# One tile in 32 fetched row by row by SyncE and ScalarE instead of by a GpSimd gather

## The reference

```
h = max(layernorm(x), 0); x = x + sum over edges of norm * (h[src] @ W)            # layer 0
h = max(layernorm(x), 0); x = x + GRU(segment_sum(mlp([h[src], h[dst], e])), h)    # layer 1
h = max(layernorm(x), 0)
n = segment_sum(h[src], dst);  x = x + max(((1 + eps) h + n) @ W1 + b1, 0) @ W2 + b2   # layer 2
h = max(layernorm(x), 0)
m = segment_sum(h[src], dst) / max(count, 1)
x = x + max(m @ Wl.T + bl + h @ Wr.T, 0)                                           # layer 3
```

## Time and profile before

| | us |
|---|---|
| median of three runs | 11380.71 |
| the profiled execution | 11306.17 |
| its span, first to last instruction | 11304.4 |
| GpSimd busy | 7460.0 |
| TensorE busy | 5949.6 |
| VectorE busy | 3267.7 |
| ScalarE busy | 659.7 |
| layer two's edge stage, about 6281 to 8714 | 2433 |
| layer three's edge stage, about 8800 to 11251 | 2451 |

### The profile page before, as it was taken

How to read it: one execution, slowest core, us unless ns; L and a number is a source line. 1 busy time by engine, 2 the same in 40 slices (tenths; PEclk the granted TensorE clock), 3 DMA queues, 4 the chain that set the end, 5 groups by cost and what they waited for, 6 DMA issues and landing times. The chain is left out here.

```text
span 11304.4 us, 126194 instructions
## 1 busy us (share of the span) xinstructions
PE 5949.6 (53%) x34165; PEld 5515.0 (49%) x34166; DVE 3267.7 (29%) x4802; ACT 659.7 (6%) x1678; POOL 7460.0 (66%) x6808
## 2 busy tenths in 40 slices
PE   6566656666656777777777333333334333333334
PEld 5555555665656777777777322222223222222224
DVE  9343434334333323222233311111112211111111
ACT  3000000000001000000001000000000000000000
POOL 1888888888875555555654666666665566666665
PEclk6555555555556666666667655555556655555555
DMA  2333333333342111111111111111111111111111
GB/s 71 20 20 20 20 20 20 20 20 20 20 53 52 34 33 34 34 34 34 34 34 24 29 23 23 23 23 23 23 23 20 31 23 23 23 23 23 23 23 29
DMA packets 714529, 310.35 MB, mean 27 GB/s; under 512 B 623117, under 2 KB 627231, under 8 KB 714079
## 3 DMA queue, kind: packets, MB, share of 16 engines
q0 software_dynamic: 398640, 218.14, 16.1%
q1 hardware_dynamic: 314252, 90.77, 3.8%
q10 hardware_dynamic: 1572, 0.67, 0.0%
HBM read 223.75 MB, written 85.30 MB: 27 GB/s over the span
## 5 line engine op out<-in xcount | busy, mean ns | idle before, releaser
L969 POOL DMA_INDIRECT h_rows<-h_tab,idx x3322 | 3159.8, 951 | 1799.7 <-issue 960.3
L1521 PE MATMUL ps_seg<-hot,h_rows 128*64 128x128 f32 x6656 | 1475.9, 413 | 3231.8 <-DVE hot L1406 2979.7
L769 POOL DMA_INDIRECT parts_tab<-total,row_at x1661 | 2559.2, 1541 | 689.1 <-issue 491.2
L1521 PEld LDWEIGHTS ps_seg<-hot,h_rows 128*64 128x64 f32 x6656 | 1321.5, 220 | 3373.5 <-DVE hot L1406 1757.7
L969 POOL DMA_INDIRECT a_rows<-a_tab,idx x1661 | 1579.6, 951 | 1136.7 <-DVE pre L1119 564.7
L1450 DVE TENSOR_TENSOR acc_t<-acc_t,ps_seg 64x128 f32 x416 | 116.4, 280 | 3568.9 <-remote 1386.3
L1141 PE MATMUL ps_seg<-hot,act_rows 128*65 128x128 f32 x3328 | 752.3, 411 | 352.3 <-ACT act_rows L1214 256.7
L1141 PEld LDWEIGHTS ps_seg<-hot,act_rows 128*65 128x65 f32 x3328 | 660.8, 222 | 385.4 <-issue 375.9
L681 PE MATMUL ps_dst<-identb,relb 128*128 128x128 bf16 x1672 | 215.9, 310 | 1075.4 <-DVE relb L615 1075.4
L681 PEld LDWEIGHTS ps_dst<-identb,relb 128*128 128x128 bf16 x1672 | 161.0, 141 | 1111.5 <-DVE relb L615 1107.7
L697 PE MATMUL ps_tot<-msg,same 128*128 128x64 f32 x3328 | 647.8, 376 | 98.4 <-issue 98.4
(11 more groups left out here) (186 smaller groups left out, 5959.4 us busy)
## 6 DMA issues: line engine op xcount, KB each, us to landing
h_rows<-h_tab,idx POOLq DMA_INDIRECT x3322
edge<-edge_t SPq DMA_DIRECT2D x208, 132.0 KB
parts_tab<-total,row_at POOLq DMA_INDIRECT x1661
a_rows<-a_tab,idx POOLq DMA_INDIRECT x1661
parts_tab<-acc_t SPq DMA_DIRECT2D x3, 3360.0 KB
idx<-src_steps SPq DMA_DIRECT2D x624, 4.0 KB
u_win<-u_tab SPq DMA_DIRECT2D x208, 32.0 KB
b_win<-b_tab SPq DMA_DIRECT2D x208, 32.0 KB
```

The lines of the kernel that those rows point to most:

```text
L769: pool.indirect_dma_start(parts_tab[:, :], bass.IndirectOffsetOnAxis(ap=row_at[:, b, k:k + 1], axis=0), total[:, b, k, :], None, compute_o ...
L969: pool.indirect_dma_start(dest[:, r, k, :], None, table[:, :], bass.IndirectOffsetOnAxis(ap=idx[:, r, k:k + 1], axis=0)).then_inc(landed[r ...
L1521: last = pe.matmul(ps_seg[0:F, b, 0, :], rows_of[:, r, k, :], hot[:, b, k, :], start=(k == 0), stop=(k == K - 1))
```

## The change

One tile of each turn, tile 0 of the fourth slot (r = 3, k = 0), is no longer gathered by GpSimd. Its 128 rows are fetched by 128 transfers of 256 bytes each, one for each partition: partitions 0 to 63 by SyncE, 64 to 127 by ScalarE. They go to the same place, h_rows[:, 3, 0, :].

The source numbers of these tiles (52 x 128) are loaded in the first stage, multiplied by 256 (the bytes in a row) on VectorE, and stored in a table. In each of the two layers this table is loaded as one row of 6656 numbers, `wanted`, on one partition. For each group of eight rows the issuing engine loads eight registers from it, and then issues eight transfers, each from the byte offset in its register.

Both engines wait, once in a turn, until the last step of the turn before is done (seg_done at 4i), since that step used the ring's fourth slot. SyncE's order in a turn is: 16 rows, the index load of the next turn for slot 0, 16 rows, slot 1, and so on; the index loads of the first turn stand ahead of all. ScalarE issues its 64 rows after the first activation of the turn in layer two; in layer three 32 rows stand after the first activation and 32 after the second. TensorE, before the fourth step, waits for four more semaphores (two for each issuing engine), and for seven gathers in place of eight.

```diff
+SINGLE_R, SINGLE_K = RING - 1, 0
+SINGLE_GROUP = 8
+ROW_BYTES = 4 * F
...
+                    sp.dma_start(singles[:, :], src_singles).then_inc(singles_in, 16)
...
+                    sp.wait_ge(singles_placed, 1)
+                    sp.dma_start(single_tab, singles_at[:, :]).then_inc(singles_stored, 16)
...
+                    dve.wait_ge(singles_in, 16)
+                    dve.tensor_scalar(singles_at[:, :], singles[:, :], float(ROW_BYTES), None,
+                                      ALU.mult).then_inc(singles_placed, 1)
...
                     for k in range(tiles_of(s)):
+                        if (r, k) in singles:
+                            continue
                         pool.indirect_dma_start(
...
+        def single_rows(eng, kind, wanted, table, dest, turn, parts, in_place):
+
+            flat = table.bitcast(U8).rearrange("(a n) f -> a (n f)", a=1)
+            for first in range(parts.start, parts.stop, SINGLE_GROUP):
+                _, offsets = nc.values_load_multi_w_load_instructions(
+                    wanted[0:1, bass.ds(turn * P + first, SINGLE_GROUP)], engines=[kind], min_val=0,
+                    max_val=(NP - 1) * ROW_BYTES,
+                    skip_runtime_bounds_check_because="identifiers of nodes are smaller than the table")
+                for p, offset in enumerate(offsets):
+                    eng.dma_start(dest[first + p:first + p + 1, SINGLE_R, SINGLE_K, :].bitcast(U8),
+                                  flat[0:1, bass.ds(offset, ROW_BYTES)]).then_inc(in_place, 16)
...
                     def _(sp):
-                        load_indices(sp, idx, idx_in, landed)
+                        def load_index(i, r):
+
+                            hold(sp, landed[r], (LANDED - 16 * (r == SINGLE_R)) * i)
+                            sp.dma_start(idx[:, r, :], src_steps[bass.ds(RING * i + r, 1), :, :]
+                                         .rearrange("s p k -> p (s k)")).then_inc(idx_in[r], 16)
+
+                        for r in range(RING):
+                            load_index(0, r)
+                        sp.wait_ge(singles_stored, 16)
+                        sp.dma_start(wanted[:, :], single_tab.rearrange("(a t) p -> a (t p)", a=1)).then_inc(wanted_in, 16)
+                        sp.wait_ge(wanted_in, 16)
+                        for i in first_loop_last(sp, TURNS):
+                            hold(sp, seg_done, RING * i)
+                            for r in range(RING):
+                                single_rows(sp, mybir.EngineType.SP, wanted, table, rows_of, i, sp_parts[r],
+                                            sp_rows_in[r // 2])
+                                if not (isinstance(i, int) and i == TURNS - 1):
+                                    load_index(i + 1, r)
...
+                                hold(act, seg_done, RING * i)
+                                single_rows(act, mybir.EngineType.Activation, wanted, table, rows_of, i, act_parts[0],
+                                            act_rows_in[0])
                                 hold(act, pair_turned, i + 1)
...
+                                if r == SINGLE_R:
+                                    for h in range(2):
+                                        pe.wait_ge(sp_rows_in[h], 512 * i + 512)
+                                        pe.wait_ge(act_rows_in[h], 512 * i + 512)
+                                    pe.wait_ge(landed[r], (LANDED - 16) * i + 16 * (tiles_of(s) - 1))
```

More of the change, by code:

```diff
@@ L11 @@
 I32 = mybir.dt.int32
+U8 = mybir.dt.uint8
 P = 128
@@ L255, in gnn_kernel @@
             eps_c = sb(ph, "eps_c", [P, 1])
+            singles = sb(ph, "singles", [TURNS, P], I32)
+            singles_at = sb(ph, "singles_at", [TURNS, P], I32)
             ps_deg = psum(ph, "ps_deg", [P, 512])
@@ L959, in load_indices, with gather_rows @@
                                  ).then_inc(idx_in[r], 16)
-        def gather_rows(pool, idx, idx_in, table, dest, landed, used):
+        def gather_rows(pool, idx, idx_in, table, dest, landed, used, singles=()):
             for i in first_loop_last(pool, TURNS):
@@ L1387, in edge_sums @@
                                                  "own_kept"))
+                wanted = sb(ph, f"wanted{layer}", [1, TURNS * P], I32)
+                wanted_in = sem(f"l{layer}_wanted_in")
+                sp_parts = [slice(q * 16, q * 16 + 16) for q in range(4)]
+                act_parts = [slice(64, 96), slice(96, P)]
+                sp_rows_in = [sem(f"l{layer}_sp_rows_in{h}") for h in range(2)]
+                act_rows_in = [sem(f"l{layer}_act_rows_in{h}") for h in range(2)]
                 idx_in = [sem(f"l{layer}_idx_in{r}") for r in range(RING)]
@@ L1395, in _ @@
                     def _(sp):
-                        load_indices(sp, idx, idx_in, landed)
+                        def load_index(i, r):
[14 more added lines that the diff above has]
+                                    load_index(i + 1, r)
                     @block.gpsimd
                     def _(pool):
-                        gather_rows(pool, idx, idx_in, table, rows_of, landed, seg_done)
+                        gather_rows(pool, idx, idx_in, table, rows_of, landed, seg_done, ((SINGLE_R, SINGLE_K),))
                     @block.vector
@@ L1466, in _ @@
                         def _(act):
+                            act.wait_ge(wanted_in, 16)
                             for i in first_then_loop(act, TURNS):
@@ L1484, in _ @@
                                                      ACT.Copy).then_inc(pair_t_ready, 1)
+                                single_rows(act, mybir.EngineType.Activation, wanted, table, rows_of, i, act_parts[1],
+                                            act_rows_in[1])
                                 hold(act, own_done, i + 1)
@@ L1518, in _ @@
                                 need(pe, acc_done, s - 1)
-                                pe.wait_ge(landed[r], LANDED * i + 16 * tiles_of(s))
+                                if r == SINGLE_R:
+                                    for h in range(2):
+                                        pe.wait_ge(sp_rows_in[h], 512 * i + 512)
+                                        pe.wait_ge(act_rows_in[h], 512 * i + 512)
+                                    pe.wait_ge(landed[r], (LANDED - 16) * i + 16 * (tiles_of(s) - 1))
+                                else:
+                                    pe.wait_ge(landed[r], LANDED * i + 16 * tiles_of(s))
                                 for k in range(K):
```

9 lines of the change are left out of this document (8 added, 1 removed).

## The result

The changed kernel takes 12533.9 us (median of 4 runs, 12502.1 to 12542.2), the kernel before beside it 11380.2 (4 runs): ratio 1.1006, 95% interval 1.0984 to 1.1027. Slower, as forecast, and inside the range; but the loss is 1154 us where 635 were forecast. Its profiled execution took 12526.7 us, with a span of 12524.9.

What follows compares the result with a forecast made beforehand. GpSimd, with two short TensorE stops, was taken to pace each 46.84 us turn; a 52.9 us row chain adds 6.06 x 104 = 630, plus 5 small, giving 11941 profiled, 12016 us on the runs' scale; range 11270 to 13100.

Steps and rivals of the forecast that it cites:

- The bound of the kernel before: Layers two and three: GpSimd paces each turn, 40.2 us of gathers plus two stops for TensorE, 46.8 us.
- The chain that replaces it: Each turn of the changed kernel: start 0.6, SyncE issue 46.3, landing 2.0, TensorE's fourth step 4.0; 52.9 us.
- SyncE's issue: SyncE's share of a turn: 64 rows at 0.62 us, 4.4 of register loads, 2.2 of index loads; 46.3 us.
- The clean row: Undisturbed issue of one row, read from similar transfers: 0.52 us on SyncE, 0.57 on ScalarE.
- the slow kind: SyncE transfers while GpSimd gathers: up to 1.95 us a row; only a small part included in the 0.62 taken.
- The register load: Before each group of eight rows: 0.29 us load, 0.16 register work, 0.1 gaps; 0.55 us, eight times 4.4.
- The signs named beforehand: Gathers every 1.256 us, one GpSimd wait of 5 us or more a turn, rows over 0.55 apart, stages 2700 to 2800 us.
- ScalarE no cheaper than SyncE: ScalarE's 64 rows a turn at the same 0.62 us: 44.1 us and one or two, neither engine much ahead.
- The rival of the slow manner: SyncE's rows at 1.95 us while GpSimd gathers: turn 78 us, or about 65 if half the time; chance 0.18.
- The rival of hidden rows: Rows at 0.42 to 0.50 us stay hidden behind GpSimd: turn 45.6 us at best, about 11320 us; chance 0.17.
- The late index: Next turn's first index load, queued behind SyncE's rows: GpSimd waits some 4.5 us, covered by time it loses anyway.
- The break-even: Row price at which the change turns from paying to costing: 33.6 us left for 64 rows, 0.525 us each.

Runs made afterwards that it cites:

- No rows: Changed kernel with the 128 single rows neither issued nor waited for, their tile left out of the sums: 11259.9 us, ratio 0.9882.
- few gathers: Changed kernel with GpSimd gathering one tile a step instead of eight, all 128 rows still issued: 10075.4 us, ratio 0.8896.
- With twice the time for them: Changed kernel with the single tile fetched by rows only every second turn, over two turns, into its own place: 11367.9 us, ratio 1.0037 to the kernel before.
- index first: Changed kernel with SyncE's next-turn index loads for slots 0 to 2 issued ahead of its end-of-turn wait and rows: 12360.5 us, ratio 1.0837.
- the last run: Changed kernel with row fetches only every second turn, plus GpSimd waiting for the previous slot's landing before slots 0 and 2: 10347.1 us, ratio 1.0361.

## Why the prediction was right, and where its size was not

- *The bound of the kernel before* (GpSimd, 40.2 us of gathers and two stops): right. No rows gave 45.8 us where 45.6 were worked out.
- *The chain that replaces it* (start, SyncE's issue, landing, fourth step): right as a chain. In the turn shown: 0.7 (VectorE's add at 8046.29 to 8047.02) + 52.4 + 1.3 + 3.7 = 58.1 us, against 0.6 + 46.3 + 2.0 + 4.0 = 52.9. Landing was taken 0.7 too long, from a transfer of 128 KB.
- *The step that was mis-sized is SyncE's issue, the price of a row.* It was 6 us a turn too low (46.3 against 52.3), the fixed links some 1 us too high (6.6 against 5.5), so the turn came out at 52.9 instead of 57.8: 104 x 4.9 = 510, and 12534 - 12016 is 518. Its two halves were both wrong. The clean row was taken too dear: 0.52 and 0.57 us were the clean rows it started from, where "few gathers" has 0.32 from row to row, and 29 us for 64 rows with loads and indices, 0.45 each. And the slow kind was given "a small part", where it costs nearly as much again as the clean rows: 52.3 - 28.9 = 23.4 us a turn. The register load was put at 0.55 with its arithmetic, from the earlier trace rows, whose loads fetch one number; a TENSOR_LOAD of eight alone is 0.69 to 0.75 us. That the forecast came as near as it did is in part luck: two errors of opposite sign.
- *The signs named beforehand*: gathers every 1.256 us, and one long wait of GpSimd a turn for the end of the fourth step, came. The two stages did not last 2700 to 2800 us but some 2990, and the rows were not evenly over 0.55 us apart: within a group of eight SyncE's median is 0.37 and its mean 0.70, ScalarE's 0.32 and 0.53.
- *ScalarE no cheaper than SyncE* (44.1): wrong. It took 38.7 us; beside gathers the same rows cost it less than SyncE.
- *The rival of the slow manner* (0.18) named what makes the rows dear, "while GpSimd gathers", and priced it too high: 65 to 78 us a turn. It had taken every row of a 40 us stretch, or half of them, at 1.95. The forecast and this rival were one mechanism at two strengths, and the measured turn lay between. The evidence for it was on record: the earlier trace rows, with a maximum of 1397 ns; in the changed kernel it is 1396.
- *The rival of hidden rows*: the clean price that it needs was met in two runs, with few gathers, and beside full gathers on the last chip. On the chips with the hold it was not. With twice the time for them, the rows were hidden there and the gain of the half gather still did not come.
- *The late index*: right, with twice the count. GpSimd waited 4.9 us (8055.44 to 8060.30) at the first slot as forecast, and 4.2 us again at the second, all of it covered; index first moved 1.1 us a turn.
- *The break-even*, 0.525 us a row: consistent. It is a price without loads and indices, and the clean one is 0.32, well under it. The only clean rows beside full gathers are those of the last run, where a turn had 31.5 gathers and its waits; the changed kernel was not run there.

## What to carry to other kernels

An engine that looks idle may still not issue at its clean price, and that price can differ by chip: measure the row's price beside the engine that will be busy, not in another stage, and take the spread of an instruction (333 ns median, 1397 maximum) as a cost and not as noise. Small transfers moved off a busy GpSimd have to be hidden whole before they pay: here 128 issues stood against 1.256 us. And a turn that waits for a chain of issue is read with one sum: the longer of the issuing chains and the fixed links behind it.

## What the runs showed of the hardware that was not expected

- While GpSimd runs a second burst of eight gathers directly after the first, TensorE's step does not end (drain 12 to 13 us for 3.3), and SyncE and ScalarE nearly stop (6 and 1 rows in 9.8 us). A drain of GpSimd between bursts, a pause of 2.5 to 2.6 us, ends it in all 416 steps; a wait for the landing, some 2.2 us, in most but not all. SyncE's register work is slow in it as well as its transfers: 0.70 us for a MOVE of 29 ns. The mechanism stays open. The page of the changed kernel counts 46 packets in the instruction queue q14, fewer than its turns, which speaks against the fetching of instructions but does not rule it out; no run tests it.
- In the one kernel traced on the last chip it does not occur, and rows issued beside full gathers have their clean price. The kernel before takes 9986 us there, not 11327 to 11389. A ratio measured on one chip need not hold on another.
- A drain of GpSimd behind eight gathers takes 2.5 to 2.6 us.
- One transfer of 256 bytes takes SyncE 228 and ScalarE 224 ns to issue, where the transfers of the earlier trace rows take 333. The rule weighed in the prediction, from the Trainium skill (DMA: Bandwidth & Descriptors, Issuing engines are not separate DMA queues), that issue time is usually small beside the transfer, does not hold for rows this small: 64 issues take 29 us clean and 52 beside the gathers of the changed kernel, with 1.3 us of landing behind them.
